# Experts 1 to 7 of a mixture-of-experts layer on collected tokens instead of on all tokens

## The reference

```python
logits = flat_x @ W_router + b_router
top_vals, top_idx = jax.lax.top_k(logits, 2)
router_weights = softmax(logits with all but the two best at -inf)
for e in range(8):
    h = relu(flat_x @ W1[e] + b1[e])           # 512 x 256 by 256 x 1024
    y = h @ W2[e] + b2[e]                      # 512 x 1024 by 1024 x 256
    final_output += y * (router_weights[:, e] * chosen(e))[:, None]
```

## Time and profile before

| | us |
|---|---|
| median of 3 runs (970.67 to 972.51) | 971.53 |
| the profiled execution | 974.7 |
| its span, first to last instruction | 972.9 |
| PE / DVE / ACT / POOL busy | 930.1 / 733.4 / 502.7 / 557.7 |
| granted TensorE clock, mean | 0.989 |

### The profile page before, as it was taken

The page is one execution under the profiler, slowest core; times in us unless marked ns, Lnnn a source line. Parts: engine busy times, 40 slices in busy tenths (PEclk is TensorE's granted clock), DMA queues, the critical chain, the costliest instruction groups (busy, mean ns, idle before and its releaser), DMA issues.

```text
span 972.9 us, 16568 instructions
## 1 busy us (share of the span) xinstructions
PE 930.1 (96%) x6116; PEld 799.2 (82%) x6116; DVE 733.4 (75%) x1147; ACT 502.7 (52%) x856; POOL 557.7 (57%) x590
## 2 busy tenths in 40 slices
PE   6999999999999999999999999999997699999998
PEld 3568888888888888888888888888786587888887
DVE  5658787787977978778797787865776667888776
ACT  3556556665666555656566665664452333344332
POOL 5729678768948957876894895720000442444440
PEclk9999999999999999999999999999999799999999
DMA  5872112212211211221221121101005022222200
GB/s 161 284 243 62 45 57 59 63 42 60 64 38 52 71 39 58 58 63 40 59 67 39 52 70 37 56 4 65 1 2 173 11 85 78 87 87 88 87 1 22
DMA packets 75087, 66.42 MB, mean 68 GB/s; under 512 B 7920, under 2 KB 71680, under 8 KB 75008
## 3 DMA queue, kind: packets, MB, share of 16 engines
q1 hardware_dynamic: 75008, 65.37, 22.3%
HBM read 57.48 MB, written 7.86 MB: 67 GB/s over the span
## 4 chain that ended last, share of the span: by engine, by line
PE 85%; DVE 11%; ACT 3%; issue 1%; DMA 0%; SPq 0%; POOL 0%; DVEq 0%; ACTq 0%
PE sps L1194 28%; PE scp L1212 9%; PE scp L1214 9%; PE scp L1213 9%; PE scp L1409 5%; PE sps L1395 4%; PE wps L1395 4%; PE scp L1410 3%; DVE u_sb L910 2%; PE wps L1239 2%; DVE st L875 1%; PE sps L1307 1%; PE scp L1162 1%; PE sps L1148 1%; DVE pt_lo L900 1%
## 5 line engine op out<-in xcount | busy, mean ns | idle before, releaser
L1212 PE MATMUL scp<-cn,pt_hi 128*128 128x258 f32 (+1 forms) x832 | 240.0, 288 | 4.4 <-DVE pt_lo L900 3.7
L1213 PE MATMUL scp<-cn,pt_hi 128*128 128x256 f32 (+1 forms) x832 | 235.5, 283 | 0.0
L1214 PE MATMUL scp<-cn,pt_lo 128*128 128x258 f32 (+1 forms) x832 | 235.2, 283 | 0.0
L900 DVE TENSOR_TENSOR pt_lo<-st,pt_hi 128x512 fp32r<-128x512 f32 (+1 forms) x208 | 196.1, 943 | 6.8 <-ACT pt_hi L670 6.8
L661 ACT ACTIVATE st<-sps 128x512 f32<-128x512 f32 (+1 forms) x208 | 123.4, 593 | 149.1 <-PE sps L1194 148.2
L875 DVE TENSOR_TENSOR st<-st,mbc 128x512 f32<-128x512 f32 (+1 forms) x208 | 156.7, 754 | 38.9 <-ACT mbc L684 38.4
L1194 PE MATMUL sps<-qk_hi,ct_hi 128*128 128x512 f32 (+1 forms) x416 | 168.4, 405 | 11.3 <-DVE cmax L886 5.8
L667 ACT ACTIVATE st<-st 128x512 f32<-128x512 f32 (+1 forms) x208 | 130.3, 627 | 88.4 <-DVE st L875 87.8
L1212 PEld LDWEIGHTS scp<-cn,pt_hi 128*128 128x128 f32 (+1 forms) x832 | 157.3, 189 | 14.9 <-DVE pt_lo L900 6.6
L1194 PE MATMUL sps<-qk_hi,ct_lo 128*128 128x512 f32 (+1 forms) x416 | 164.4, 395 | 0.0
L1213 PEld LDWEIGHTS scp<-cn,pt_hi 128*128 128x128 f32 (+1 forms) x832 | 157.7, 190 | 7.5 <-issue 0.2
(11 more groups left out here) (209 smaller groups left out, 1447.6 us busy)
## 6 DMA issues: line engine op xcount, KB each, us to landing
w_raw<-W SPq DMA_DIRECT2D x16, 1024.0 KB, 7.5
raw<-ctx_t SPq DMA_DIRECT2D x96, 128.0 KB, 2.2
raw<-ctx_n SPq DMA_DIRECT2D x96, 128.0 KB, 2.0
raw<-qk_scratch SPq DMA_DIRECT2D x56, 128.0 KB, 2.0
qk_scratch<-stage_b SPq DMA_DIRECT2D x4, 896.0 KB, 4.8
qk_scratch<-stage_a SPq DMA_DIRECT2D x4, 896.0 KB, 4.6
wq_sb<-w_q SPq DMA_DIRECT2D x1, 1024.0 KB, 5.8
wkt_sb<-w_kt SPq DMA_DIRECT2D x1, 1024.0 KB, 8.3
```

The costliest lines, as they stand in the source:

```text
L900: dve.tensor_tensor(pt_lo[0:rows(j), r, :], st[0:rows(j), par, j, :], pt_hi[0:rows(j), r, :].bitcast(F32), ALU.subtract).then_inc(lo_ok, 1)
L1212: pe.matmul(scp[:, t, 0:D + 2], hi, cn[0:rows(j), j, 0:D + 2], start=j == 0, stop=False)
L1213: pe.matmul(scp[:, t, 0:D], hi, cn[0:rows(j), j, D + 2:CNW], start=False, stop=False)
L1214: ins = pe.matmul(scp[:, t, 0:D + 2], lo, cn[0:rows(j), j, 0:D + 2], start=False, stop=j == SJ - 1)
```

## The change

Expert 0 stays as it is. Experts 1 to 7 no longer run over all 512 tokens:

- SP clears two tables in DRAM, 8 x 512 rows of 1 KB each (`clear_rows`, four DMAs in slot 29 of the attention).
- The second layer norm is kept in `xln`. Each chain makes one-hot rows of its two experts; PE ranks the tokens of each expert by matmuls with triangular and all-one matrices; DVE makes from them the row number of each token and choice (`routes`), once for tiles 0 to 2 and once for tile 3, and finds which experts have more than 256 tokens (`over_done`).
- POOL writes each token's `xln` row to its two row numbers with eight indirect DMAs (`scatter`).
- Ten passes of 256 rows follow: experts 1 to 7, then three that take the second 256 rows of an over-full expert, whose number SP reads from memory (`load_unit`, `rows_of`). A pass loads its rows, transposes them on PE (`transpose_x`), splits them (`take_xt`, `xt_low`), runs `h_z` and `y_z`, and stores 256 rows of y (`take_y`, `finish_y`, `store_y`). Each pass has its own weights, loaded and split as before.
- At the end POOL fetches each token's two rows by eight indirect DMAs (`gather`), DVE multiplies them with the weights and adds them to `x_sb`, and the result is stored.

```diff
+            def clear_rows():
+                sp.wait_ge(zero_ok, 1)
+                for dst in (xg_dram, yg_dram):
+                    n = ROWS // P
+                    v = dst.rearrange("(n p) d -> p n d", p=P)
+                    for h in range(DT):
+                        sp.dma_start(v[:, :, h * P:(h + 1) * P],
+                                     zrow[:].unsqueeze(1).broadcast_to((P, n, P))).then_inc(zeroed, 16)
...
+                    if of == 0 and u == ZERO_AT:
+                        clear_rows()
...
+            def load_unit(w):
+                s = w % 2
+                if w >= 2:
+                    sp.wait_ge(w_ready, low_count(w - 2))
+                if w == NE:
+                    sp.wait_ge(over_ok, OVER_NO["unit"])
+                    for i in range(NOV):
+                        over_e.append(sp.value_load(unit_i[0:1, i:i + 1], min_val=0, max_val=NE - 1))
+                        sp.dma_start(b1_over[:, i, :], b1[:, bass.ds(over_e[i], 1), :]).then_inc(b1_in, 16)
+                e = bass.ds(w if w < NE else over_e[w - NE], 1)
+                sp.dma_start(w1_raw[:, s, :, :],
+                             W1[e, :, :].rearrange("o (t p) n -> p (o t) n", p=P)).then_inc(w1_in[s], 16)
+                sp.dma_start(w2_raw[:, s, :, :],
+                             W2[e, :, :].rearrange("o (t p) n -> p (o t) n", p=P)).then_inc(w2_in[s], 16)
+            def load_x(z):
+                if z == 0:
+                    sp.wait_ge(scattered, 16 * 2 * MT)
+                if z >= 2:
+                    sp.wait_ge(xt_pe, z - 1)
+                sp.dma_start(xg_sb[:, z % 2, :, :],
+                             xg_dram[rows_of(z), :].rearrange("(a p) d -> p a d", p=P)).then_inc(xg_in[z % 2], 16)
+            def store_y(z):
+                sp.wait_ge(yb_ok, z + 1)
+                if z >= NE:
+                    sp.wait_ge(yg_out[(z - 1) % 2], 16 * ((z - 1) // 2 + 1))
+                sp.dma_start(yg_dram[rows_of(z), :].rearrange("(a p) d -> p a d", p=P),
+                             ybuf[:, z % 2, :, :]).then_inc(yg_out[z % 2], 16)
+            load_unit(0)
+            load_unit(1)
+            load_unit(2)
+            load_x(0)
+            load_x(1)
+            for z in range(NZ):
+                if z + 3 < NU:
+                    load_unit(z + 3)
+                if z + 2 < NZ:
+                    load_x(z + 2)
+                store_y(z)
...
+            def scatter(m):
+                if m == 0:
+                    pool.wait_ge(zeroed, 16 * 2 * DT)
+                pool.wait_ge(route, ROUTE_NO["slot_b" if m == MT - 1 else "slot_a"])
+                pool.wait_ge(chain_dve[m], DVE_NO["ln2"])
+                for j in range(2):
+                    pool.indirect_dma_start(
+                        xg_dram, bass.IndirectOffsetOnAxis(slot_i[:, m, j:j + 1], 0),
+                        xln[:, m, :], None).then_inc(scattered, 16)
...
-            low_weights(0, 1, 0)
+                low_weights(0, part)
+            low_weights(1, 0)
             chain_rstd(3, 2)
+            for m in range(MT - 1):
+                scatter(m)
+            low_weights(1, 1)
+            scatter(MT - 1)
+            for part in range(2, 4):
+                low_weights(1, part)
+            for w in range(2, NU):
+                for part in range(4):
+                    low_weights(w, part)
+            for i in range(2):
+                pool.wait_ge(yg_out[i], 16 * (NZ // 2))
+            for m in range(MT):
+                gather(m)
...
+            def take_xt(z):
+                act.wait_ge(xt_pe, z + 1)
+                act.wait_ge(h_ok, FT * max(2, z + 1))
+                act.activation(xT_hi[:, z % 2, :, :], scp[:, 2 * (z % 2), :].rearrange("p (t q) -> p t q", t=DT),
+                               ACT.Copy).then_inc(xt_hi_ok, 1)
+            def take_y(z):
+                act.wait_ge(y_ok, unit_done(z + 1))
+                if z >= 2:
+                    act.wait_ge(yg_out[z % 2], 16 * (z // 2))
+                b0 = 2 * (z % 2)
+                act.activation(ybuf[:, z % 2, :, :], scp[:, b0:b0 + 2, 0:D], ACT.Copy).then_inc(ya_ok, 1)
+            def relu_z(z, f):
+                p = z + 2
+                act.wait_ge(h_ok, p * FT + (f + 1))
+                act.wait_ge(hl_ok, p * FT + (f - 1))
+                act.activation(h_f[:, f % 2, 0:TK], hbank(f)[:, 0:TK], ACT.Relu,
+                               bias=b1_unit(z + 1, f)).then_inc(hf_ok, 1)
+            take_xt(0)
+            for z in range(NZ):
+                if z == NE - 1:
+                    act.wait_ge(b1_in, 16 * NOV)
                 for f in range(FT):
+                    relu_z(z, f)
+                    if f % 2 and z + 2 < NU:
+                        high_weights(z + 2, f // 2)
+                if z + 1 < NZ:
+                    take_xt(z + 1)
+                take_y(z)
...
+                    after("topf")
+                    for j in range(2):
+                        done(dve.tensor_scalar(onehot[:, m, j, :], eidx[:], topf[:, m, j:j + 1], None, ALU.is_equal))
+                    after("oh1")
+                    done(dve.tensor_tensor(cnt[:, m, :], onehot[:, m, 0, :], onehot[:, m, 1, :], ALU.add))
...
+            def routes(m0, m1, x):
...
+                dve.wait_ge(rank_ok, 1 if m0 == 0 else 2)
+                dve.scalar_tensor_tensor(out=pos[:, m0:m1, :], in0=eidx[:].unsqueeze(1).broadcast_to((P, n, NE)),
+                                         scalar=float(TOK), in1=bank, op0=ALU.mult, op1=ALU.add).then_inc(route, 1)
+                after("pos")
+                dve.tensor_tensor(both[:, m0:m1, :, :], onehot[:, m0:m1, :, :],
+                                  pos[:, m0:m1, :].unsqueeze(2).broadcast_to((P, n, 2, NE)), ALU.mult).then_inc(route, 1)
+                after("both")
+                dve.tensor_reduce(slotf[:, m0:m1, :], both[:, m0:m1, :, :], AX.X, ALU.add).then_inc(route, 1)
+                after("sum")
+                dve.tensor_copy(slot_i[:, m0:m1, :], slotf[:, m0:m1, :]).then_inc(route, 1)
             for n in range(2 * FT):
                 if n < FT:
                     split_h(0, n)
                 if n in LAST:
                     chain(MT - 1, LAST[n])
+                if n == 5:
+                    routes(0, MT - 1, "a")
+            routes(MT - 1, MT, "b")
+            def over_done(ins):
+                ins.then_inc(over_ok, 1)
+            over_done(dve.scalar_tensor_tensor(out=overe[:], in0=hbank(2)[:, NE:2 * NE], scalar=float(TK), in1=eidx[:],
+                                               op0=ALU.is_gt, op1=ALU.mult))
...
+            def split_z(z, f):
+                p = z + 2
+                dve.wait_ge(hf_ok, p * FT + (f + 1))
+                dve.wait_ge(y_ok, p * FT + (f + 1 - FT))
+                dve.tensor_copy(h_hi[:, f, 0:TK], h_f[:, f % 2, 0:TK]).then_inc(hh_ok, 1)
+                dve.wait_ge(hh_ok, p * FT + (f + 1))
+                dve.tensor_tensor(h_lo[:, f, 0:TK], h_f[:, f % 2, 0:TK], h_hi[:, f, 0:TK].bitcast(F32),
+                                  ALU.subtract).then_inc(hl_ok, 1)
...
+            xt_low(0)
+            for z in range(NZ):
                 for f in range(FT):
+                    split_z(z, f)
+                if z + 1 < NZ:
+                    xt_low(z + 1)
+                finish_y(z)
+            dve.wait_ge(yc_ok, MT)
+            for m in range(MT):
+                dve.wait_ge(gathered[m], 32)
+                for j in range(2):
+                    if j == 1:
+                        dve.wait_ge(add_ok, 2 * m + 1)
+                    dve.scalar_tensor_tensor(out=x_sb[:, m, :], in0=ytok[:, m, j, :], scalar=tw2[:, m, j:j + 1],
+                                             in1=x_sb[:, m, :], op0=ALU.mult, op1=ALU.add).then_inc(add_ok, 1)
...
+            def rank(m):
+                bank = scp[:, 0, m * NE:(m + 1) * NE] if m < MT - 1 else hbank(2)[:, 0:NE]
+                for before in range(m):
+                    pe.matmul(bank, all_ones[:], cnt[:, before, :], start=before == 0, stop=False)
+                return pe.matmul(bank, before_it[:], cnt[:, m, :], start=m == 0, stop=True)
...
+            def transpose_x(z):
+                pe.wait_ge(xg_in[z % 2], 16 * (z // 2 + 1))
+                if z < 2:
+                    pe.wait_ge(yc_ok, 2 * (z + 1))
+                else:
+                    pe.wait_ge(yb_ok, z - 1)
+                for dt in range(DT):
+                    for a in range(2):
+                        n0 = (dt * 2 + a) * P
+                        ins = pe.transpose(scp[:, 2 * (z % 2), n0:n0 + P],
+                                           xg_sb[:, z % 2, a, dt * P:(dt + 1) * P], ident[:])
+                ins.then_inc(xt_pe, 1)
+            def h_z(z, f):
+                if f == 0:
+                    pe.wait_ge(w_ready, low_count(z) + DT)
+                    pe.wait_ge(xt_lo_ok, z + 1)
+                pe.wait_ge(hf_ok, (z + 2) * FT + (f - 3))
+                n = 0
```

(54 more changed lines are left out.)

203 lines of the change are left out of this document (126 added, 77 removed).

## The result

The changed kernel takes 1034.76 us (median of 4 runs, 1033.76 to 1035.41), the kernel before on the same chip 971.1 (4 runs, 969.96 to 972.51): ratio 1.0654, interval 1.0635 to 1.0672. It is slower, as predicted (1027.5, range 1000 to 1050), and 7.3 us slower than the forecast. The profiled execution took 1035.41, its span 1033.7, against 974.7 and 972.9 of before: 60.8 us of span.

What follows compares the result with a forecast made beforehand. It took PE to bound the kernel before (experts 1 to 7, 156.1 us) and POOL-DVE exclusion to pace the passes. Terms 25 + 9 + 8 + 14 = 56; 974.7 + 56 - 3.2 = 1027.5 us, range 1000 to 1050.

Steps and rivals of the forecast that it cites:

- zero fill: Table clearing on SP's queue delays context loads and POOL's splits before the score group of 136.76: plus 9, 0 to 24.
- entry: Ahead of the first pass: added small DVE instructions, rank matmuls and x's low part, plus 8 us, between 3 and 12.
- passes: Ten passes replacing experts 1 to 7: 9 x 18.8 + 11.7 = 181 us against 156.1, plus 25.
- end: After PE's last work: y copy and store, eight gathers at 1.1, landing 2.0, additions, output; sum 17.6, plus 14.
- the lock alone: In each pass, exclusive POOL and DVE times 15.0 us plus 2.4 at the boundary: 17.4 us.
- PE alone: PE's work in one pass, both products and four transposes: 11.7 us.
- The clock: In each pass's PE gap the clock falls to 0.50; four closing y pairs take 1.4 us longer, 18.8 a pass.
- The scatters: Eight POOL issues at 1.1 from 793, x loaded by 815, hidden by additions before 821; otherwise 3 to 4 us.
- PE's pace of 11.7 a pass: Rival for the passes: POOL's splits slip between DVE's instructions, PE keeps the pace; 963.5 us, chance 0.12.
- Long issues of 2.4 for indirect DMAs: Rival: issues held by DVE or simply long, only the end pays, 10 more, 1038 us; chance 0.12.
- The rival with the clock at 1.00: In the passes the lock holds but the clock does not fall: 168 us of passes, 1015 us; chance 0.20.

Runs made afterwards that it cites:

- e4: Changed kernel plus 28 matmuls into an unused bank in PE's gap ahead of y tile 6 in nine passes: 1019.16 us.
- e3: Changed kernel with POOL making the weights' low parts for 8 columns only in all passes but the first: 969.74 us, ratio 0.9983 to before.
- e11: Changed kernel with the same four clearing DMAs in the same place, written in 1 KB pieces (half the packets): 1030.97 us.
- e2: Changed kernel; in the passes ACT writes h's high part and an in-place relu, DVE subtracts reading PSUM and one SBUF operand: 974.33 us.
- e8: e5 with the last rank matmuls behind both halves of expert 0's small h, where DVE also subtracts from PSUM: 964.03 us.
- e1: Changed kernel with the four clearing DMAs split into sixteen of a quarter size, one per slot from slot 29: 1025.65 us.
- e9: e5 with one gather per tile, four indirect DMAs instead of eight, the second choice left out of the output: 960.15 us.
- e5: Changed kernel with the edits of e1 and e2 together: 966.8 us, ratio 0.9959 to before.
- e10: e8 with the last tile's gate-weight step on DVE moved ahead of the last ranks: 963.31 us, ratio 0.9911 to before.
- e12: e10 with nine small DVE instructions on over-full experts moved behind the h splits and twelve filler matmuls in PE's gap: 965.8 us.

## Why the prediction was right

The direction and the mechanism of the passes held. The four terms of the sum, by spans:

| term | predicted | measured |
|---|---|---|
| zero fill | 9 | 10.9 |
| entry | 8 | 8.3 |
| passes | 25 | 25.6 |
| end | 14 | 15.9 |
| sum, before rounding | 56 | 60.8 |

- **Passes.** 181 us predicted, 1014.56 - 832.82 = 181.7 measured; the lock alone 17.4 a pass predicted, 17.09 in e4; with the clock 18.8 predicted, 18.9 in the timeline; PE alone 11.7 predicted, 11.64 in e3. The prediction added four POOL subtractions and eight DVE pairs as if each took its turn. In fact POOL's subtractions run in pairs, and DVE gets one instruction in between them, so the whole wait shows as four long DVE instructions a pass. Two of the eight pairs end with POOL's rows and add little, but POOL idles longer while the chain over DVE and ACT runs: in e4 it is busy for 9.6, idle for 2.54 in the middle of the pass and for 4.95 at its border. The total of 17.4 came out nearly right although the parts lie elsewhere.
- **The clock.** The fall was where it was put, behind the last subtraction (885 to 889). e4 prices it at 15.6 us in all, against 9 x 1.4 = 12.6 by the prediction: the four closing y pairs take 0.64 each for 0.35 (1.2), and the low clock reaches six matmuls into the next first product (1.29 us for 0.72, 0.6 more), which the prediction had only as a possibility.
- **The fill.** It lasted from 94.5 to about 127 (124 predicted) and POOL resumed at 127.56 (126). PE's two waits are 8.0 together, as the 8 to 9 said, though not in one place and with POOL faster than taken (1.35 per tile while DVE idles, not 1.75). The missing term is the clock: 0.70 and 0.67 in the two stretches of 5 us behind the waits, 5 x 0.30 + 5 x 0.33 = 3.1 or 3.2. I had counted it in the passes and not here. Not foreseen either is that SP itself is held: 21 us for issuing the four DMAs, and 8.56 for the next two. That its length came out nearly as forecast (some 32 us for 31) is in part luck: it was counted in packets, and e11 shows that mostly bytes set it.
- **Entry.** 8.3 against 8, and the agreement is luck: four parts of it are off and cancel. Taken at the same points, less the fill's 10.9: (1) the small h of expert 0 begins at 810.49 - 10.9 = 799.6, against 801.23 before, 1.6 earlier and not 1.8 later. The 2.4 us that POOL had taken from the layer norm (2.48, now 0.41) lay on the chain; the prediction had seen that they come free and put them at nothing, because PE was the pace there. (2) The two halves and the ranks take 8.7 us for 5.3: 3.4 more, where 1.5 stood. The ranks are 1.7 of it; the rest is the clock in the second half, 4.33 for 2.63. (3) The 13 small DVE instructions (814.9 to 817.1), for which 2.7 - 1.3 = 1.4 stood, are hidden beside that second half, but the cast behind them waits for POOL, 2.86 us for 0.43 in the earlier trace rows: 2.4 more in all. The prediction had named these low parts of POOL and asked only when they end, not whom they hold. (4) From there to the first h tile it is 4.2 more, where 2.7 stood.
- **End.** 1.25 per gather (0.95 busy and 0.30 between) and not 1.1: 1.2 more; landing 2.8 and not 2.0: 0.8 more. The scatters cost nothing, as said: their last issue is at 817.27 and x's loads are issued at 819.77, ahead of the transposes of 829.
- **The other 2.5 us** of the miss of the median are in the base: before's profiled execution was 3.2 over its median, so 3.2 came off; after's was 0.65 over its own.

The rivals: PE's pace of 11.7 a pass is what e2 and e3 give once the exclusion is gone, so it was a real alternative and the earlier trace rows ruled it out rightly. Long issues of 2.4 for indirect DMAs fell: 0.95 to 1.22. The rival with the clock at 1.00 said that the fall needs a long gap. In the passes it had one, of 4 us; ahead of the first pass it fell with none (see the open point below).

The Trainium skill, SBUF — State Buffer, section A bandwidth-pool intuition that's wrong, has about 3.1 us for a DMA issued from GpSimd beside a DVE copy. No scatter here stood beside a long DVE copy, so that price is neither shown nor refuted: the scatter of 817.27 began inside a cast of 0.43 us and took 1.04, and the same one in e8, where that cast is gone, 0.97.

The Trainium skill, SBUF — State Buffer, section Who interferes with whom, has the port held for a whole instruction. The runs agree (2.23 us for a cast of 0.28 under a subtraction of 2.4) and show more: 4.37 us for a 128x1 multiplication is a wait for two POOL instructions in a row.

Open: the clock ahead of the first pass. In the kernel before it is 1.00 in every stretch of 2 us from 800 to 834. In the changed kernel and in each variant that keeps the ranks between the halves of the small h, it falls to 0.50 about 1 us (0.7 to 1.5) behind the sixteen rank matmuls of 8 columns: in the changed kernel these run from 812.96 to 814.86 and the clock falls near 816, though PE is busy without a gap from 808 to 820. The prediction had a fall only behind gaps. That the ranks are the cause is not shown, since no run takes them out. When the clock comes back varies: at 822 in the changed kernel, at 810 to 812 in e1 and e9, only after 828 in e5, whose first pass begins 2.9 us later than that of e9. No run isolates what decides it.

## What to carry to other kernels

When a change halves the work of the bounding engine, list what does not halve with it. Here the split of weights on POOL and its exclusion with DVE were hidden under PE and became the pace; the change paid only once DVE read one operand from PSUM and the fill was spread (966.8 us in e5; 963.3 in e10, 0.89% under the kernel before, and 71 under the change as made). What a DVE instruction on SBUF alone costs while POOL runs large ones back to back was not set by its size here (4.37 us for 128x1): look at what DVE has queued at that moment, small bookkeeping too. A bulk DMA on the queue that feeds the pipeline is better cut into pieces between the loads: same bytes, 10.9 us less here.

## What was not expected of the hardware

- Two POOL subtractions back to back let one DVE instruction in after the first, in the passes (2.23, then 2.49 us). At the entry none got in before both had ended: a cast in the changed kernel (2.86) and in e5 (3.44), one multiplication in e8 (4.37), the first of three small ones in e12 (5.31, issued 0.6 before the pair is recorded to begin). In the passes the second subtraction's input became ready while the first ran; at the entry both were ready before. Whether that is the reason was not tested.
- Issuing the four DMAs of 2 MB (4096 pieces each) holds SP for 0.5, 5.5, 6.0 and 8.8 us, and the next two short loads for 7.3 and 1.3; with a quarter of the size it is 0.43 to 1.04 each in e1.
- 8.4 MB written from one SBUF row: 284 to 293 GB/s in pieces of 512 B, 341 to 350 in pieces of 1 KB, in stretches of 5 us with the DMA engines full in both.
- An indirect DMA of 128 rows of 1 KB costs POOL 0.94 to 1.04 us (the first scatter 1.22) and 0.30 until the next, read or write; the last of eight lands after 2.8.
- The clock fell to 0.50 behind sixteen matmuls of 8 columns without a gap in PE's work (see Open above).
